# Spreading the s1 rows of chunks 1 and 2 by DMA in place of TensorE and ScalarE

## The reference

```python
def _L0_gnn_ref(input1, input2, adj, a1, a2):
    e = input1 @ a1 + (input2 @ a2).T
    e = jnp.where(e > 0, e, 0.2 * e)
    att = jnp.where(adj > 0, e, NEG)
    att = jax.nn.softmax(att, axis=1)
    deg = jnp.sum(adj, axis=1, keepdims=True)
    att = att * deg
    att = GAMMA * att + (1.0 - GAMMA) * adj
    return att @ input2
...
x = x + _L0_gnn_ref(_layernorm(x, axis=-1), L0_gnn_input2, adj, L0_gnn_a1, L0_gnn_a2)
x = x + _L0_ffn_ref(_layernorm(x, axis=-1)[None], L0_ffn_weight, L0_ffn_bias)[0]
```

## Time and profile before

| | us |
|---|---|
| median of 3 runs | 377.66 |
| lowest and highest | 376.27, 379.8 |
| the profiled execution | 377.19 |
| its span, first to last instruction | 375.3 |
| TensorE busy | 361.4 |
| VectorE busy | 314.3 |
| ScalarE busy | 256.7 |
| GpSimd busy | 147.4 |

### The profile page before, as it was taken

One profiled execution on the slowest core, in us unless ns is written; L12 is line 12 of the kernel. 1 busy time (PEld: TensorE's weight loads), 2 busy tenths in 40 slices (PEclk: granted clock), 3 DMA queues, 4 the chain that ended last, 5 costly groups with the idle time before them and its releaser, 6 DMA issues.

```text
span 375.3 us, 8925 instructions
## 1 busy us (share of the span) xinstructions
PE 361.4 (96%) x3226; PEld 317.6 (85%) x3226; DVE 314.3 (84%) x790; ACT 256.7 (68%) x628; POOL 147.4 (39%) x258
## 2 busy tenths in 40 slices
PE   7689999999999999999999999999999999999992
PEld 6578888888888888888888888888888888888881
DVE  5998989979999978879787887988788797999842
ACT  4799896696686686592939659292966929897100
POOL 4595723806161613417071452707144250701111
PEclk9999999999999999999999999999999999999997
DMA  7999959591949592946739193773909330110001
GB/s 246 205 215 201 215 113 190 84 205 13 207 75 195 77 208 49 168 85 118 151 49 211 24 180 75 122 146 61 207 18 177 78 42 2 19 14 14 17 2 32
DMA packets 18631, 42.32 MB, mean 113 GB/s; under 512 B 3732, under 2 KB 9880, under 8 KB 18584
## 3 DMA queue, kind: packets, MB, share of 16 engines
q0 software_dynamic: 9216, 33.56, 48.1%
q1 hardware_dynamic: 9368, 8.15, 8.7%
HBM read 73.14 MB, written 2.11 MB: 201 GB/s over the span
## 4 chain that ended last, share of the span: by engine, by line
PE 87%; DMA 4%; DVE 3%; POOL 3%; issue 1%; SPq 0%; ACT 0%; DVEq 0%; POOLq 0%
PE acc_u L715 26%; PE acc_v L718 26%; PE acc_y L697 24%; DMA adj_all<-adj 3%; PE acc_v L697 3%; PE acc_u L697 2%; PE acc_y L686 2%; PE small L680 2%; DVE plus L1115 2%; DMA plus<-in 1%; PE turned L654 1%; DVE weights_y L1106 1%; POOL pre_h L398 1%; PE acc_u L686 0%; POOL b_rest L440 0%
## 5 line engine op out<-in xcount | busy, mean ns | idle before, releaser
L514 ACT ACTIVATE steep<-s_bc,steep_s 128x256 bf16<-128x256 f32 x512 | 218.0, 518 | 13.7 <-DVE plus L936 6.9
L718 PE MATMUL acc_v<-weights_v,minus 128*128 128x258 f16 x896 | 198.2, 272 | 0.0
L715 PE MATMUL acc_u<-weights_u,plus 128*128 128x258 f16 x896 | 198.2, 273 | 0.0
L697 PE MATMUL acc_y<-weights_y,adj_all 128*128 128x257 f16 x896 | 101.5, 273 | 0.7 <-DMA adj_all<-adj 0.7
L697 PEld LDWEIGHTS acc_y<-weights_y,adj_all 128*128 128x128 bf16 x896 | 86.7, 97 | 12.8 <-DMA adj_all<-adj 1.2
L718 PEld LDWEIGHTS acc_v<-weights_v,minus 128*128 128x128 bf16 x896 | 87.1, 97 | 11.4
L715 PEld LDWEIGHTS acc_u<-weights_u,plus 128*128 128x128 bf16 x896 | 86.7, 97 | 11.9
L936 DVE TENSOR_TENSOR plus<-adj_all,steep 128x2048 bf16<-128x2048 bf16 x64 | 80.3, 1255 | 17.5 <-ACT steep L514 17.5
L939 DVE TENSOR_TENSOR minus<-adj_all,plus 128x2048 bf16<-128x2048 bf16 x64 | 78.8, 1232 | 2.2
L413 POOL TENSOR_SCALAR post_var<-post_mv 128x2 f32<-128x2 f32 x15 | 3.2, 213 | 165.8 <-DVE post_mv L1048 165.8
L528 ACT ACTIVATE num<-acc_u,ac 128x129 f32<-128x129 f32 x32 | 11.4, 363 | 76.2 <-PE acc_u L715 74.6
(11 more groups left out here) (132 smaller groups left out, 325.7 us busy)
## 6 DMA issues: line engine op xcount, KB each, us to landing
adj_all<-adj POOLq DMA_DIRECT2D x64, 512.0 KB, 10.9
x_in<-x SPq DMA_DIRECT2D x16, 128.0 KB, 5.3
plus<-in SPq DMA_DIRECT2D x4, 512.0 KB, 5.6
out<-late SPq DMA_DIRECT2D x15, 128.0 KB, 5.0
s_bc<-s_rows SPq DMA_DIRECT2D x13, 128.0 KB, 8.6
s_rows<-pre_s SPq DMA_DIRECT2D x13, 1.0 KB
out<-late SPq DMA_DIRECT2D x2, 64.0 KB, 2.6
wt_sb<-w_t SPq DMA_DIRECT2D x1, 64.0 KB, 4.6
```

Source lines behind the costliest of these rows:

```text
L514: ins = nc.scalar.activation(steep[:, h, k, :].rearrange("q (t p) -> q t p", t=TILES), s1_tiles[b], ACT.Relu, bias=steep_s2[:, jt:jt + 1], ...
L697: ends[t] = nc.tensor.matmul(acc[t][:, 0:width], left[:, jt, cols(t)], right[:, jt, :, :].rearrange("p a b -> p (a b)")[:, 0:width], start ...
L715: last_u = nc.tensor.matmul(acc_u[t][:, 0:2 * WC], plus[b][:, jt, cols(t)], w_u[:, jt, :, :].rearrange("p a b -> p (a b)"), start=(jt == 0 ...
L718: last_v = nc.tensor.matmul(acc_v[t][:, 0:2 * WC], minus[b][:, jt, cols(t)], w_v[:, jt, :, :].rearrange("p a b -> p (a b)"), start=(jt == ...
```

## The change

SPREAD goes from 3 to 1, so that only chunk 0 goes by TensorE and ScalarE. The two calls of `spread` and the call of `copy_spread` for chunk 1 go out of the lists (that of chunk 2 goes by SPREAD), and SyncE stores and reads back the rows of chunks 1 and 2 as it does those of the later ones. GpSimd makes the row sums of chunk 1 between its requests of adj for chunks 2 and 3. SyncE requests x of chunk 1 when the first quarter of adj of chunk 1 is there, not the second, and x of chunk 2 behind the store and the broadcast of chunk 1, with no wait for adj of chunk 2. VectorE does `pre_start(1, 1)` ahead of `low_u(1)` and `pre_start(2, 0)` ahead of `masks(0, 3)`. Its wait for the exponents of the chunk before becomes one for the first step of that chunk's row sums.

```diff
--- before.py
+++ after.py
@@ -38,7 +38,7 @@
 IN2_FLOOR = 16.0
 NEG = 9e15
 GEN = 31
-SPREAD = 3
+SPREAD = 1
 AHEAD = 3
 
 
@@ -300,7 +300,8 @@
 
             def load_s1(n, b):
                 sp.wait_ge(s1_stored[b], landed(n, b))
-                sp.wait_ge(steep_done, 4 * n - 4)
+                if inner(n - 1):
+                    sp.wait_ge(steep_done, 4 * n - 4)
                 sp.dma_start(s1_bc[b][:, :], s1_rows[n].partition_broadcast(P)).then_inc(s1_landed[b], 16)
 
             sp.dma_start(a_row, a_pair.unsqueeze(0)).then_inc(a_landed, 16)
@@ -308,11 +309,11 @@
             for q in range(QUARTERS):
                 sp.dma_start(in2_f[:, q * QJ:(q + 1) * QJ, :], in2[:, q]).then_inc(in2_landed[q], 16)
             store_s1(0, 0)
-            sp.wait_ge(adj_landed[1][1], 16)
+            sp.wait_ge(adj_landed[1][0], 16)
             sp.dma_start(x_in[1][:, :, :], x[1]).then_inc(x_landed[1], 16)
-            sp.wait_ge(adj_landed[2][0], 16)
+            store_s1(1, 1)
+            load_s1(1, 1)
             load_x(2, 0)
-            store_s1(1, 1)
 
             for c in range(CHUNKS):
                 b = c % 2
@@ -453,10 +454,10 @@
             factor_columns()
             factors(0, 0, True)
             load_adj(2)
+            row_sums(1, 1)
             load_adj(3)
             nc.gpsimd.tensor_scalar(minus_ident[:, :], ident[:, :], -1.0, 1.0, ALU.mult, ALU.mult)\
                 .then_inc(ident_negated, 1)
-            row_sums(1, 1)
             factors(1, 1, False)
 
             for c in range(CHUNKS):
@@ -596,7 +597,6 @@
             high_v(3)
             high_u(3)
             sign_tests(0, 3, 0)
-            copy_spread(1, 1)
             exps(0, 0)
 
             def slot(c, f):
@@ -805,13 +805,11 @@
             y_quarter(2, 0)
             y_quarter(2, 1)
             y_quarter(2, 2)
-            spread(1, 1)
             masked_quarter(0, 2)
             y_quarter(2, 3)
             masked_quarter(0, 3)
             for q in range(QUARTERS):
                 y_quarter(3, q)
-            spread(2, 0)
 
             def slot(c, f):
                 b = f % 2
@@ -913,7 +911,7 @@
 
                 dve.wait_ge(x_landed[b], landed(n, b))
                 if inner(n):
-                    dve.wait_ge(pre_pool, PRE * n)
+                    dve.wait_ge(pre_pool, PRE * (n - 1) + 1)
                 for t in range(TILES):
                     nc.vector.bn_stats(pre_st[:, t, :], x_in[b][:, t, :]).then_inc(pre_stats, 1)
                 wait_apart(dve, pre_stats, TILES * (n + 1))
@@ -1172,19 +1170,20 @@
             value_u(1)
             for t in range(TILES):
                 linear_part(0, t, 0)
+            pre_start(1, 1)
             low_u(1)
             low_v(1)
             masks(0, 1, 0, 0)
             value_u(2)
             for t in range(TILES):
                 linear_part(1, t, 1)
-            pre_start(1, 1)
             low_u(2)
             low_v(2)
             value_u(3)
             masks(0, 2, 0, 0)
             low_u(3)
             low_v(3)
+            pre_start(2, 0)
             masks(0, 3, 0, 0)
 
             def slot(c, f):
@@ -1204,8 +1203,6 @@
                     for t in range(TILES):
                         linear_part(2, t, 0)
                     masks(1, 0, 1, 1)
-                if not inner(c):
-                    pre_start(2, 0)
                 if c >= RANGE_FROM and c < RANGE_FROM + QUARTERS:
                     range_check(c - RANGE_FROM)
                 if not ahead(c, 1):
```

## The result

The changed kernel takes 385.25 us (median of 4 runs, 384.37 to 387.88) against 378.48 for the kernel before beside it: a ratio of 1.021, with a 95% interval of 1.017 to 1.0249. A second measurement on another chip (experiment 3) has 1.0155 (1.0097 to 1.0213). The profiled execution takes 384.47, its span is 382.7 against 375.3, 7.4 us more. From 100 us on TensorE is busy all the time at full speed, as before. The loss is all in the opening.

The account below looks back on a forecast made before the run. TensorE, busy 361.4 of 375.3 us, bounds the kernel; only the opening has room. Spreads −0.9, adj landing −0.1, wait for x of chunk 2 +1.2 sum to +0.2: 377.9 us, range 376.2 to 380.6.

Parts of the forecast that it names:

- x of chunk 2 lands at 47.0: Opening, SyncE's queue: x lands 0.9 us behind the broadcast's 46.1, making TensorE wait 1.2 us before chunk 0's last masked quarter.
- the upper bound of 50.5: Opening: latest landing of x of chunk 2, 31.8 + 7.9 + 9.9 + 0.9; TensorE would then wait 4.7 us.
- 31.8: Opening, GpSimd: row sums of chunk 1 take 1.6 us and end at 31.8, when the store is issued.
- where I took 5.7: Opening, SyncE: chunk 1's broadcast follows its store by 5.7 us, between bounds 3.3 and 7.9, so requested at 37.5.
- a bound of 7.9 from the broadcasts in the stream: Opening: upper bound from chunk 1's store to its broadcast, adding a full adj stream's effect, 8.6 against 4.0 us.
- 45.77: Opening: TensorE waits if x of chunk 2 lands later than this, 48.39 − 2.62; at 47.0 it waits 1.2 us.
- −0.9 for the spreads: Opening, TensorE's chain: removing two spreads of 0.45 us each gains 0.9 us, if what follows is ready.
- 5.3 us, so I take 0: Opening: x of chunk 1 takes the median 5.3 us, lands at 28.6; `linear_part(1)` ends at 37.16 against 37.39, costing 0.
- a rival with a chance of 0.10: Opening, x of chunk 1 late: 7.1 us, not 5.3; TensorE loses about 1.3 at `linear_part(1)`, total 379.2; chance 0.10.
- Each is 0: Slots: later x of chunk 3, weights and bias, slightly sooner chunk 4 adj, and `pre_start`'s weaker wait each cost 0.
- That ScalarE's signs don't bind: Opening, ScalarE: signs of chunk 1 start at 46.13, about when the broadcast lands (46.1); nothing counted.
- The page that was weighed: Opening DMAs: about 2 us fixed means x by about 38, no wait; ring order means x cannot pass the broadcast.

Follow-up runs that it names:

- experiment 3: The changed kernel with no edit, measured again on the chip of a version with 20 matmuls on constants in TensorE's wait: 383.26 us, ratio 1.0155.
- experiment 1: The changed kernel, but SyncE requests x of chunk 2 ahead of the store and broadcast of chunk 1: 377.95 us, ratio 1.0018.
- experiment 9: The changed kernel with x of chunk 2 requested between the store and the broadcast of chunk 1: 378.45 us, ratio 1.0021.
- experiment 10: The kernel before with chunk 2's row through memory, weights and bias behind x of chunk 2, x of chunk 3 ahead of chunk 2's store: 377.25 us, ratio 0.9984.
- the first one with the filler: The changed kernel with 20 unread matmuls on constants on TensorE ahead of chunk 0's last masked quarter, first of two measurements: 382.35 us, ratio 1.0132.
- experiment 8: The kernel before with only x of chunk 1 requested earlier, VectorE's work on it ahead of `low_u(1)`, and the weaker wait: 378.43 us, ratio 1.0031.
- experiment 6: The kernel before with only the row of chunk 2 sent through memory (SPREAD = 2, no `spread(2, 0)`): 380.90 us, ratio 1.0108.
- experiment 2: The changed kernel with VectorE's work on x of chunk 2 back behind the masks of chunk 1: 383.92 us, ratio 1.016.
- experiment 7: The kernel before with only `pre_start(2, 0)` ahead of `masks(0, 3)` and the weaker wait in `pre_start`: 377.13 us, ratio 1.0008.
- experiment 5: The changed kernel with x of chunk 1 requested on chunk 0's last adj quarter and x of chunk 2 ahead of store and broadcast: 377.73 us, ratio 1.0024.
- experiment 4: The changed kernel, but GpSimd requests the adj quarters of chunk 3 only when x of chunk 2 has landed: 379.41 us, ratio 1.0065.

## Why the prediction was wrong

I predicted 377.9 us in a range up to 380.6, and the time is 385.25. The mechanism stood in the prediction, with its place: VectorE held by x of chunk 2 ahead of the last quarter's masks, TensorE behind it. Its size was wrong.

- **The failed term: "x of chunk 2 lands at 47.0".** It lands at 52.3, beyond the upper bound of 50.5, and the wait costs 5.4 us in place of 1.2. The difference comes in three parts. The row sums are done at 34.3, not 31.8 (2.5 us): GpSimd itself was 1.5 behind (29.58 against 28.04) after an early half-speed stretch of TensorE, and its power operation took 1.57 us in place of 0.73. The store took 7.7 us where I took 5.7 (2.0). And from the broadcast's request to x's landing it is 10.2 us where I had 9.5 (0.7). For the store I had a bound of 7.9 from the broadcasts in the stream and went to the middle by another row. In all nine profiles with this store beside the stream its broadcast is requested 7.1 to 8.4 us behind it, near that bound. Both transfers stayed within their bounds in the change. The sum of the bounds failed because it starts from 31.8, to which I had given no range. The rest of the sum holds: by its rule a landing at 52.3 makes a wait of 52.3 − 45.77 = 6.5 us, and with −0.9 for the spreads and 1.7 for the clock that is 7.3, where the span grew by 7.4.
- **A term that was missing: the clock.** I priced the wait by its length alone. The 1.7 us at half speed behind it weren't in the sum or in a rival, and neither is an earlier stretch near 15 us. That one isn't the change's own: the profiles of experiments 1, 9 and 10 and the first one with the filler have one between 9 and 25 us too. The kernel before has runs at a mean clock of 0.983, which may hold one as well; no trace shows it.
- **x of chunk 1: "5.3 us, so I take 0".** It took 7.1 us, which was a rival with a chance of 0.10 and a price of 1.3. Experiment 8 has its part alone at 1.0031, about 1.2 us. The size of that rival was right, its place wasn't: I had TensorE wait for `linear_part(1)` ahead of acc_y of chunk 2, and it waits one piece earlier, for the `plus` of the second masked quarter (1.34 us in experiment 8, 0.35 in the change). `linear_part(1)` did end after 37.4, at 39.0. In the change this doesn't add to the 7.3 above: VectorE came to x of chunk 2 at 47.1 and had to wait for it anyway. I had the right row in hand: 7.1 was what x of chunk 2 took in the same full stream, and 5.3 the median of requests made in slots with emptier queues.
- **"Each is 0", for the requests moved further back.** In the change this was right, but not for a reason that I had given: it is VectorE's new order that sends the store of chunk 2 early enough. Without that order the broadcast of chunk 2 holds TensorE 2.4 us in experiment 6, which is 3.6 us slower than the kernel before, and 3.4 in experiment 2. I had judged the burst of adj for chunk 4 as going "a little sooner" and never asked what would be in front of the broadcast as it starts.
- **Right:** both spreads cost 0.45 each and are gained; VectorE's new order costs nothing by itself (experiment 7); the slots are as long as before. That ScalarE's signs don't bind, although the broadcast came 3.4 us later than I had it, is in part luck: TensorE was held longer by x. With x out of the way they cost it 0.7 us in experiment 5.
- **The page that was weighed.** By the Trainium skill, "DMA: Bandwidth & Descriptors", section "Anatomy of one DMA", a DMA has about 2 us fixed; the section has this from DMAs that GpSimd issues, and these are SyncE's. In the stream none of these came near that: the store took 7.7 us for 1 KB. Without the stream it holds better: x took 1.9 us in experiment 1, and the broadcast and x 3.0 and 2.9 in experiment 4. By the ring order of "Queues, rings and completion order" x could not pass the broadcast, and it didn't, by 2.8 us (49.5 to 52.3). The trace agrees with the taking of turns between queues as well: from 46 to 47 us it has 44 packets of the adj stream and 45 of SyncE's queue. But the ring order is worth only these 3 us or so. The larger part of the lateness is SyncE's wait for the store, as experiment 9 shows.

What stays open: in the change about 3 us pass between the request of the broadcast at 42.07 and the first packets of SyncE's queue at about 45, beside the stream. Without the stream, in experiment 4, it is 1 to 2 us. No run shows what they wait for. Nor does a run take the store's 128 pieces away alone; their share is read from the packets of experiment 9.

## What to carry to other kernels

A transfer that depends on another one's landing makes the issuing queue wait, and everything behind it in that queue is requested a whole latency later: put the independent requests first. Take the latency of a moved transfer from rows made under the load that it will meet, not from the median of all, and count the requests that stand in front of it on its queue (about 3 us each in this stream). And when a wait is put on the path of a busy TensorE, add the half-speed stretch that may follow it.

## What the runs showed of the hardware

- A store of 1 KB from 128 partitions took 7.7 us beside a full stream of adj (8.4 in experiment 4), and 3.3 us from issue to the next request with nearly empty queues. x of 128 KB took 7.1 in that stream: there the 144 packets of a request counted, and not its bytes. SyncE's queue got 40 to 63 packets per us beside about as many of adj.
- The same broadcast of 128 KB took 3.0 us without the stream, 7.4 in it, and 13.6 when three other requests and a burst of adj went ahead of it. x of 128 KB took between 1.9 and 10.8 us.
- Behind idle stretches of 5.2 and 4.5 us TensorE's granted clock was at half (1.2 GHz) in both profiles of the change, and it wasn't with matmuls on constants in that stretch. It was also at half behind 3.4 us in experiment 2 and 2.4 us in experiment 6, but not behind the 1.7 us near 36 us of experiment 2. In the opening it fell in five profiles and not in others with much the same idle time: the change idles 2.3 us until 13.7 and is at half from 14.3 on, the kernel before idles 2.2 us until 13.5 and stays at full speed. In the profile of experiment 1 it was at half from 11 to 24 us:

```profile
...
11.00:24.00 13.00, 10.57 (x50) 7.59 (x49) 9.60 (x48) 7.52 (x20) 5.57 (x9) 0.50 1.03 201
...
```
